# The projection of the edge part as three products of split operands, and the quotients of the attention part spread over the next round

## The reference

```
qkv  = 1x1 products of x with wq, wk, wv          (1536 channels)
pw   = 1x1 groups of a 5x5 depthwise conv of qkv  (1536 channels)
per head (128 of them, 8 channels each), on relu(q), relu(k), v:
  scores = [v, 1] k^T ;  out = scores q ;  out = out[:-1] / (out[-1] + eps)
y = proj_kernel (512 x 1024) times out, batch norm, + x
edges: Sobel, Laplace and diagonal stencils of y, sqrt/abs, four 1x1 branches,
       a gate from the channel means, a 1x1 fusion, layer norm, relu, + y
```

## Times and the profile before

| | us |
|---|---|
| median of 3 runs | 5162.94 |
| lowest and highest | 5160.89, 5172.66 |
| the profiled execution's own time | 5166.08 |
| its span from first to last instruction | 5164.3 |
| TensorE busy | 4887.3 (95%) |
| VectorE, ScalarE, GpSimd busy | 50%, 39%, 24% |
| attention part, edge part | 0 to 3138, 3138 to 5164 |

### The profile page before, as it was taken

The page is one execution under the profiler, slowest core; times in us unless marked ns, Lnnn a source line. Parts: engine busy times, 40 slices in busy tenths (PEclk is TensorE's granted clock), DMA queues, the critical chain, the costliest instruction groups (busy, mean ns, idle before and its releaser), DMA issues. The chain is left out here.

```text
span 5164.3 us, 65339 instructions
## 1 busy us (share of the span) xinstructions
PE 4887.3 (95%) x22760; PEld 3443.6 (67%) x22760; DVE 2579.4 (50%) x3635; ACT 2023.0 (39%) x3671; POOL 1223.6 (24%) x1030
## 2 busy tenths in 40 slices
PE   8999999999999999999999997899999989998968
PEld 7887887887887888888888883344344434443423
DVE  3334334334334333333334321786688578848865
ACT  3333333333333333333333320454555455545545
POOL 2442342342342342342342330000300020011003
PEclk9999999999999999999999998999999999999969
DMA  6665666665665665665666654443334344434313
GB/s 184 197 216 203 198 211 203 198 212 202 198 213 203 198 215 203 198 214 203 198 213 203 203 185 170 139 147 123 138 123 155 108 147 131 143 118 145 110 34 116
DMA packets 390808, 893.04 MB, mean 173 GB/s; under 512 B 33488, under 2 KB 66512, under 8 KB 388240
## 3 DMA queue, kind: packets, MB, share of 16 engines
q1 hardware_dynamic: 390544, 889.18, 52.2%
HBM read 588.74 MB, written 300.32 MB: 172 GB/s over the span
## 5 line engine op out<-in xcount | busy, mean ns | idle before, releaser
L733 POOL TENSOR_TENSOR toeplitz<-taps 128x512 f32<-128x512 f32 x768 | 889.2, 1186 | 959.1 <-PE bank L441 959.1
L441 PEld LDWEIGHTS bank<-toeplitz,columns 128*128 128x128 f32 x8192 | 954.4, 192 | 13.8
L441 PE MATMUL bank<-toeplitz,columns 128*128 128x128 f32 x8192 | 955.7, 275 | 0.0
L1039 PE MATMUL bank<-att,w_proj 128*128 128x512 f32 x2048 | 906.2, 597 | 47.7 <-DMA att<-att_dram 36.6
L1039 PEld LDWEIGHTS bank<-att,w_proj 128*128 128x128 f32 x2048 | 392.1, 192 | 543.6 <-issue 505.1
L356 PE MATMUL bank<-x_hi,w_hi 128*128 128x512 f32 x1536 | 610.8, 398 | 17.1 <-DVE x_lo L600 17.1
L1383 POOL TENSOR_TENSOR centred<-centred,x_out 128x512 f32<-128x512 f32 x128 | 164.6, 1321 | 1910.2 <-ACT centred L1191 1910.2
L358 PE MATMUL bank<-x_lo,w_hi 128*128 128x512 f32 x1536 | 600.9, 391 | 0.0
L1052 PE MATMUL bank<-edge,w_branch 128*128 128x512 f32 x1024 | 503.2, 639 | 102.5 <-ACT edge L1142 102.5
L357 PE MATMUL bank<-x_hi,w_lo 128*128 128x512 f32 x1536 | 599.5, 390 | 0.0
L671 DVE TENSOR_SCALAR ckey_t<-bank 128x256 f32<-128x256 f32 x256 | 107.5, 420 | 872.0 <-PE bank L441 872.0
(11 more groups left out here) (115 smaller groups left out, 5618.9 us busy)
## 6 DMA issues: line engine op xcount, KB each, us to landing
x_sb<-in_x_tiled SPq DMA_DIRECT2D x128, 1024.0 KB, 6.4
tiles_dram<-tiles SPq DMA_DIRECT2D x128, 867.0 KB, 6.7
loaded<-tiles_dram SPq DMA_DIRECT2D x256, 433.5 KB, 4.0
inverse<-inverse_dram SPq DMA_DIRECT2D x256, 256.0 KB, 4.8
att_dram<-out_sb SPq DMA_DIRECT2D x256, 256.0 KB, 4.1
att<-att_dram SPq DMA_DIRECT2D x64, 1024.0 KB, 6.2
xb<-x_dram SPq DMA_DIRECT2D x128, 330.0 KB, 3.1
x_out<-in_x_pad SPq DMA_DIRECT2D x32, 1056.0 KB, 5.2
```

What stands on the lines that cost most here:

```text
L441: last = nc.tensor.matmul(bank[:, v * M:(v + 1) * M], columns[:, h % 2, t - T_K, v + b, a * HT:(a + TO) * HT], w[:, t, d, :], start=(d == ...
L733: last = nc.gpsimd.tensor_tensor(toeplitz[:, h % 2, t, :].rearrange("p (d o r) -> p d o r", o=HD, r=PL), tap, point, ALU.mult)
L1039: last = nc.tensor.matmul(P_BANKS[m][:, :], w_proj[:, i * HALF + k, m * P:(m + 1) * P], att[:, i, k, :], start=(i == 0 and k == 0), stop=( ...
```

## The change

**Attention, what is written.** After each `divide`, ACT rounds the quotient (`round_out`, to `out_hi`) and DVE subtracts (`split_out`, to `out_lo`, which lies where `out_sb` lay). `spill` writes both, and waits for `out_split` in place of `divided`. The mixed weights are rounded and subtracted likewise (`w_part_hi`, `w_part_lo`), by two further DVE instructions, and written as two.

**Attention, where the quotients stand.** Quotients 0 to 3 of half 1 are made in steps 4 to 7 of the next `plain`, one in a step, 4 to 7 in heads 0 to 3 of the following `conv`, and those of half 0 in heads 4 to 11. In `conv` the `divide` now stands ahead of the evacuation of k. `split_weights` moves from head 7 to head 13. The first `conv` and the second `plain` are taken out of the loop.

**Attention, memory.** The Toeplitz taps are loaded two heads at a time in place of four; `score_d` is a window on one wide row of zeros, so that one DVE instruction fills it in place of two.

**Edges.** `load_att` and `load_mixed` load both parts (two DMAs of 1 MB each in place of one), and `project` makes three products of float32r operands in place of one in float32. Some small tiles share memory with others; `w_att1` and `w_att2` are loaded again for each image, and `mean_w` is set again.

```diff
@@ attention, spill and write_w (sync)
                 def spill(it, half, j):
-                    sp.wait_ge(divided, START + at(it, half, j) + 1)
-                    sp.dma_start(dram["att"][it // HS][it % HS + HS * half][:, j * CH:(j + 1) * CH],
-                                 out_sb[:, j % 2, :]).then_inc(out_written[j % 2], 16)
+                    sp.wait_ge(out_split, at(it, half, j) + 1)
+                    for part, of in enumerate((out_hi, out_lo)):
+                        sp.dma_start(dram["att"][it // HS][it % HS + HS * half][part][:, j * CH:(j + 1) * CH],
+                                     of[:, j % 2, :].bitcast(F32)).then_inc(out_written[j % 2], 16)
@@ attention, plain (sync)
-                            if j >= 4:
-                                for i in range(2 * j - 8, 2 * j - 6):
-                                    spill(conv_of, 1, i)
-                                    if i + 2 < NCH:
-                                        load_inverse(conv_of, 1, i + 2)
+                            if j >= LATE:
+                                load_inverse(conv_of, 1, j - LATE + 2)
+                        if conv_of is not None and j >= LATE:
+                            spill(conv_of, 1, j - LATE)
                         if j + XR < NCH:
                             sp.wait_ge(qkv_ready, 3 * (NCH * it + j + 1))
                             load_x(it, j + XR)
@@ attention (scalar)
+                def round_out(it, half, j):
+                    act.wait_ge(divided, START + at(it, half, j) + 1)
+                    copy(out_hi[:, j % 2, :], out_sb[:, j % 2, :]).then_inc(out_rounded, 1)
@@ attention (vector)
+                def split_out(it, half, j):
+                    dve.wait_ge(out_rounded, at(it, half, j) + 1)
+                    nc.vector.tensor_tensor(out_lo[:, j % 2, :], out_sb[:, j % 2, :], out_hi[:, j % 2, :].bitcast(F32),
+                                            ALU.subtract).then_inc(out_split, 1)
...
                                             ALU.mult).then_inc(w_out_ready, 1)
+                    dve.wait_ge(w_out_ready, START + 2 * it + half + 1)
+                    dve.wait_ge(den_written, 16 * START + 16 * (2 * it + half + 1))
+                    nc.vector.tensor_copy(w_part_hi[:, :], w_proj[:, :]).then_inc(w_part_rounded, 1)
+                    dve.wait_ge(w_part_rounded, 2 * it + half + 1)
+                    nc.vector.tensor_tensor(w_part_lo[:, :], w_proj[:, :], w_part_hi[:, :].bitcast(F32),
+                                            ALU.subtract).then_inc(w_part_split, 1)
@@ edges, project (tensor)
-                            last = nc.tensor.matmul(P_BANKS[m][:, :], w_proj[:, i * HALF + k, m * P:(m + 1) * P],
-                                                    att[:, i, k, :], start=(i == 0 and k == 0), stop=(i == 1 and k == HALF - 1))
+                            wide, narrow = (w[:, i * HALF + k, m * P:(m + 1) * P] for w in (w_proj_hi, w_proj_lo))
+                            high, low = att_hi[:, i, k, :], att_lo[:, i, k, :]
+                            nc.tensor.matmul(P_BANKS[m][:, :], wide, high, start=(i == 0 and k == 0), stop=False)
+                            nc.tensor.matmul(P_BANKS[m][:, :], narrow, high, start=False, stop=False)
+                            last = nc.tensor.matmul(P_BANKS[m][:, :], wide, low, start=False, stop=(i == 1 and k == HALF - 1))
```

More of the change, by code:

```diff
@@ L270, in plain, with conv @@
                         load_head(h)
-                def conv(it, last):
+                def conv(it, started, last):
                     for h in range(SH):
@@ L277, in conv @@
                             load_head(h + LR)
[L278 to L281 removed]
+                        if h % 2 == 1 and (h < SH - 3 or not last):
+                            n, groups = (h + 3) // 2, SH // LT
+                            sp.wait_ge(toeplitz_ready, SH * it + LT * (n - 1))
+                            load_taps(it + n // groups, n % groups)
                         if not last and h == 1:
@@ L397, in denominate @@
                     for j in range(NCH):
-                        last = nc.tensor.matmul(DEN_BANK[:, :], score_d[:, j * P:(j + 1) * P], rows((relu_q, relu_c)[half], j),
+                        last = nc.tensor.matmul(DEN_BANK[:, :], score_d[:, P - SH * (j + 1):2 * P - SH * (j + 1)], rows((relu_q, relu_c)[half], j),
                                                 start=(j == 0), stop=(j == NCH - 1))
@@ L468, in first @@
                     plain(0, None)
+                    conv(0)
+                    plain(1, 0)
                 def steady(it):
@@ L523, in plain @@
                             round_x(it, j + 1)
+                        if conv_of is not None and j >= LATE:
+                            round_out(conv_of, 1, j - LATE)
                         key(it, j)
@@ L559, in first @@
                     plain(0, None)
+                    conv(0, False, False)
+                    plain(1, 0)
                 def steady(it):
-                    conv(it, False)
+                    conv(it, True, False)
                     plain(it + 1, it)
                 def final(it):
-                    conv(it, True)
+                    conv(it, True, True)
                     scores_to_mix(it, 1)
+                    for j in range(NCH):
+                        round_out(it, 1, j)
                 pairs(act, first, steady, final)
@@ L654, in plain @@
                                 invert(conv_of, 1)
-                            if j >= 4:
-                                for i in range(2 * j - 8, 2 * j - 6):
-                                    divide(conv_of, 1, i)
+                            if j >= LATE:
+                                divide(conv_of, 1, j - LATE)
                         if j + 1 < NCH:
@@ L661, in plain @@
                         compress(it, j)
+                        if conv_of is not None and j >= LATE:
+                            split_out(conv_of, 1, j - LATE)
                     keys_by_position(it, NCH - 2)
@@ L665, in plain, with conv @@
                     invert(it, 0)
-                def conv(it, more):
+                def conv(it, started, more):
                     for h in range(SH):
+                        if division(it, h, started):
+                            divide(*division(it, h, started))
                         dve.wait_ge(cready[T_K], SH * it + h + 1)
@@ L755, in first @@
                     plain(0)
+                    conv(0, False)
+                    plain(1)
                 def steady(it):
@@ L782, in edges @@
         work = sb("work", [P, 3, XR * W])
+        with nc.sbuf_tensor("mean_w", [P, P], F32) as mean_w:
+            pass
         sobel_h = sb("sobel_h", [P, 2, CR, W])
```

161 lines of the change are left out of this document (93 added, 68 removed).

## The result

The changed kernel takes 5238.99 us (median of 4 runs, 5225.30 to 5242.08) beside 5167.8 us for the kernel before on the same chip: 1.0133 times as long, 95% interval 1.0112 to 1.0154. The forecast was 5190, slower by 0.5%; the direction was right, the size too small by more than half. The measured time lies outside the forecast's own range (5174 to 5215) and inside the wider one (5075 to 5260). The profiled execution has a span of 5234.8 us against 5164.3, 70.5 more, where my sum had 28.

The account below looks back on a forecast made before the run. TensorE, busy 95% of the span, was taken as the bound. Terms, chiefly -120 for edges and +138 for x loads, summed to about +28 on 5166.1, 5194, or 5190 as median; own range 5174 to 5215, wider 5075 to 5260.

Parts of the forecast that it names:

- loads of x behind the writes: Attention, `plain`: x loads queue behind quotient writes, `qkv` of chunks 6 and 7 late by 4.3 and 4.9 us; +138 us.
- key at the end of `plain`, `score_d`: Attention: fourth subtraction delays the key of chunk 6, +10 us; one DVE instruction less ahead of `denominate`, -3.
- tail, and the first 4 MB: After the last round nothing hides the quotient chain, +13.5 us; doubled loads ahead of the projection's first matmul, +5.
- `split_weights`, heads, first round: Attention, `conv`: `split_weights` in head 13 no longer meets a quotient and a Toeplitz build, -4 us; quotients in heads covered, 0.
- first three chunks, first write of y: Edge part's start: three chunks of projection alone, -17 us; first write of y queues behind 1 MB more, +3.
- edge steps, fusions, one low branch: Edge part: shorter projection quarters save 120 us over steps and fusions; one more branch at the low clock, +3.
- The sign that I had named for a term set too high: Attention: waits for `x_lo` under 100 us in total would show the load term too high; about 130 us forecast.
- rival 2: Attention: granted clock falls in TensorE's waits for x; the second loss costs 2.8 us a round, +42, time 5232; chance 0.17.
- Both kinds of step: Edge loop: steps with a wait for ACT fall from 42.4 to 37.9 us, steps without from 41.20 to 36.5.
- where the table stands already: Edge loop: in the step at 41.20 us ACT's table is already loaded, its chain 6.4 us, the step 36.5.
- Rival 3: Edge part: 40.9 us is the loop's floor, set by DVE and ACT; a step gains 1.4, time 5270; chance 0.1.

Follow-up runs that it names:

- Experiment 1: Changed kernel, with SP issuing the load of x ahead of the quotient's two writes in each step of `plain`: 5099.87 us.
- experiment 9: Kernel of experiment 4 plus one small Gelu on ACT ahead of the wait for the last branch, in the edge loop's steps: 5036.99 us.
- experiment 8: Changed kernel with only the first of the projection's three products, loads and all else kept: 5231.32 us.
- experiment 5: Changed kernel with the fourth subtraction moved behind the key of chunk 6, load of x still behind the writes: 5197.58 us.
- experiment 4: Changed kernel with the load of x ahead of the writes and the fourth subtraction behind the key of chunk 6: 5067.03 us.
- experiment 6: Kernel of experiment 1 plus 10 unused matmuls on TensorE ahead of the score of chunk 6, where it waits for the key: 5077.94 us.
- experiment 2: Changed kernel with the load of x ahead of the writes in step 4 of `plain` alone: 5171.8 us.

## Why the prediction was right in direction and wrong in size

Against the sum, term by term, on the profiled executions:

| | forecast | measured |
|---|---|---|
| loads of x behind the writes | +138 | +128 |
| key at the end of `plain`, `score_d` | +7 | +36 |
| tail, and the first 4 MB | +18.5 | +19 |
| `split_weights`, heads, first round | -4 | -0.5 |
| first three chunks, first write of y | -14 | -11 |
| edge steps, fusions, one low branch | -117 | -101 |
| sum | +28 | +71 |

**The load of x** was right in mechanism and in size. The chain went as written: 4.1 and 4.5 us a round where 4.3 and 4.9 were forecast, TensorE's waits shorter than those (3.9 and 2.3 us, 93 in all, not 130), since `qkv` of chunk 6 itself ran at the lower clock in between. Experiment 1 shows that it hung on one thing, the place of an issue on SP. The sign that I had named for a term set too high, waits for `x_lo` under 100 us in total, would have misled with these 93 us: what counts is the distance from start to start.

**The key at the end of `plain`** is the step that failed: "the fourth subtraction stands right ahead of it: 15 x 0.65 = +10". The wait did grow by 0.6, from 1.54 to 2.14 us, as the earlier trace rows would have it. What I left out is what TensorE does behind it: the two scores, the transposes and the denominator ran at the lower clock. Of the 2.43 us a round, 1.05 is `qkv` of chunk 7 behind the wait for `x_lo` (rival 2's loss, smaller than its 2.8), 0.41 the longer wait less the earlier `score_d`, and 0.97 the clock behind the key, which fell there in 7 rounds. I had the clock in a rival for the long waits alone, and gave a wait of 2 us no price, since the earlier trace rows had only waits of 3.5. Moving the one subtraction gave back 33 us without and 41 us with the waits for x.

**The edge steps** have the second error. Both kinds of step were right, 38.18 and 36.78 us for 37.9 and 36.5. But I took the first kind for all three steps of an image in the loop. The first two of them come out at 39.80 and 39.91, with a branch at the lower clock behind a wait (5.65 and 2.34 us). The first of the two gains what I had forecast all the same, 18 us over four images, since before it lasted 45.1 to 45.3 in three of them, behind such a branch, and not the 42.4 that I took. The second gains 2.5 a step in place of 4.5, 8 us in all. The last steps before the fusions give 9 us in place of 13, and the first steps of the images 4 in place of 6. With a projection in the step 12 branches run long where 7 did before; I had allowed one more. My reason for the two kinds ("where the table stands already") was wrong as well: every chunk loads both tables, and the kinds differ in whether the first load stands ahead of ACT's wait or behind it (experiment 9). The numbers held, because the difference between the rows was used and not the reason.

**Rival 3**, the floor of 40.9 us, did not hold with three products. With one product it did in part: steps of 38 to 39 us at a clock of 0.81 to 0.86 (experiment 8). So the row of the steps without a projection, which I had set aside for its stretched branches, did speak of what the loop falls back to when TensorE has less to do.

**Rival 2**, the clock: it was no rival but a part of the outcome. About 16 us of it lie in `qkv` of chunk 7 and 14 behind the key. In the edge part the long branches add up to 24 us above their length at full clock, where they added 17 before, so 7 more for the 3 that I had allowed. That this rival's 5232 came within 7 us of the result is luck: its one item was set at 42 us and measured 16, and the others were not in it. In the changed kernel 14 of the 15 waits of about 3.9 us for chunk 6 were followed by a stretched `qkv` (9.98 to 11.27 us for 8.45), and 10 of 15 of the shorter second ones. The Trainium skill ("TensorE: Matmul & The Clock Gate", section "HAM oscillation — how this bites in real kernels") has it that such gaps put the array back to half clock each time. For the long waits this case nearly agrees, 14 of 15. It also shows the fall behind waits well below them: behind some 2.14 us in 7 of 15 rounds of the changed kernel and in 13 of 15 of experiment 1.

On the tables, the Trainium skill ("ScalarE: Activation LUTs", section "What ACT_TABLE_LOAD costs") gives 1283 ns for the load and about 2.66 us for a switch with its drain. The trace has the load at 1.28 us and the next activation 1.30 behind its start; no drain stands between them here, and the measurement decides.

What stays open: why the rounds of one kernel, and kernels with the same wait, differ in whether the clock falls (with the load moved in step 4 alone, 25.7 to 31.1 us for the same work), and why moving the subtraction also shortened the `qkv` ahead of it in experiment 5.

## What to carry to other kernels

When writes are made to wait for a later result, look at what else stands in the same queue behind them: here a load of x that nothing else held up cost 128 us, and two lines exchanged on SP gave 139 us back. An instruction added ahead of one for which TensorE waits can cost more than its own length: 0.6 us a round became 2.2 us with the clock behind it, so such work belongs in a place where its engine is idle, and here 2.1 us of idle stood one instruction further on. Before making TensorE's work in a loop smaller, ask how far away the next chain is: a seventh less of the projection was worth 112 us, and two thirds less of it after that was worth 8, of which the traces put 2.5 into the edge part.

## What the runs showed of the hardware that I had not expected

- A wait of TensorE for some 2.14 us was followed by work at the lower clock in 13 of 15 rounds of experiment 1, in 7 of 15 of the changed kernel, and in 59 of 90 over the six kernels that have it; the same wait at 1.54 us in 3 of 15 rounds of experiment 4 and in 4 of 60 over four kernels. The mean granted clock of the stretch behind it was 0.67 to 0.89 where it fell and 1.00 where it didn't. Matmuls of no use in the 2.14 us took 22 us off the kernel (experiment 6), where it still fell in 2 of 15 rounds.
- A kernel with such waits varies more from run to run: 5159 to 5197 in 10 runs of experiment 2, against 5065 to 5068 in 4 runs of experiment 4.
- In the loop, whose addresses come from a register, the table load of ACT started behind the semaphore wait ahead of a Gelu (1.49 us idle, then the load). In the steps written out it started ahead of that wait. One small Gelu ahead of the wait took 30 us off the kernel.
- A quarter of three float32r products lasts 5.86 us to the start of the branch behind it, and the branch 3.03 to the next quarter, where float32 had 6.87 and 3.43: the start of a branch shifts by 0.4 us against its neighbours. Together it is 8.89, for 8.87 forecast.
